# Two tap matmuls for four from a doubly laid pixel buffer, and one convolution block per tile in the small tasks' PSUM banks

## The reference

```python
x = relu(bn(conv3x3(relu(bn(conv3x3(x, sign(w1)))), sign(w2))) + x)      # L0
xn = layer_norm_over_channels(x)                                          # L1: 4 chunks of 16 channels
xz = einsum('gld,ed->gle', chunks, in_proj_w); xi, z = split(xz)
u = silu(causal_depthwise_conv4(xi) + conv_b)
delta = softplus(dt @ dt_proj_w + dt_proj_b)
h = h * exp(delta * A) + (delta * u) * B;  y = h . C                      # scan over 3136 pixels, 16 states
y = (y + u * D) * silu(z);  x = chunks + y @ out_proj_w
x = conv3x3-like block (1x1, grouped 3x3, 1x1) of x + x                   # L2
x = four directional row scans: new = cur + relu(conv9(prev))             # L3
```

## Time and profile before

| | |
|---|---|
| timed runs | median 8,072.02 us of 3 (8,068.12 to 8,075.87) |
| profiled execution | 8,083.31 us, span 8,081.5 us |
| mean granted TensorE clock | 0.943 |
| main loop (224 tiles), between its first and last scan | 707.8 to 7,368.9 us of the span |
| stages A and B, prologue | before 707.8 us |

### The profile page before, as it was taken

One profiled execution on the slowest core, in us unless ns is written; L12 is line 12 of the kernel. 1 busy time (PEld: TensorE's weight loads), 2 busy tenths in 40 slices (PEclk: granted clock), 3 DMA queues, 4 the chain that ended last, 5 costly groups with the idle time before them and its releaser, 6 DMA issues. The chain is left out here.

```text
span 8081.5 us, 108343 instructions
## 1 busy us (share of the span) xinstructions
PE 6926.8 (86%) x31741; PEld 4163.9 (52%) x31741; DVE 6670.6 (83%) x9221; ACT 5321.7 (66%) x9423; POOL 5911.0 (73%) x5627
## 2 busy tenths in 40 slices
PE   8896877878888999999789999999789999996876
PEld 8893333333334555555435555555255555554665
DVE  6776989898989898999889999999898989894111
ACT  0135777777776778777777787777677787773221
POOL 0005989898988888888888888888888888884000
PEclk9998989898989999999989999999899999998999
DMA  9774666565667565656776566656865656565001
GB/s 169 166 179 123 179 166 180 166 178 163 181 173 191 162 164 159 164 165 162 184 194 169 159 166 163 165 157 164 208 172 162 167 159 166 161 164 137 2 2 32
DMA packets 1187366, 1261.38 MB, mean 156 GB/s; under 512 B 475904, under 2 KB 1172992, under 8 KB 1186816
## 3 DMA queue, kind: packets, MB, share of 16 engines
q1 hardware_dynamic: 950784, 1177.89, 54.9%
q10 hardware_dynamic: 236032, 77.08, 4.2%
HBM read 995.47 MB, written 181.59 MB: 146 GB/s over the span
## 5 line engine op out<-in xcount | busy, mean ns | idle before, releaser
L651 POOL TENSOR_TENSOR hs<-hs,bsp 128x448 f32<-128x448 f32 x3584 | 3718.2, 1059 | 411.5 <-DVE hs L641 401.2
L641 DVE TENSOR_TENSOR_SCAN hs<-da,hs,ps 128x448 f32<-128x448 f32 x3072 | 3491.6, 1137 | 0.0
L631 DVE TENSOR_TENSOR ps<-ps,bsp 128x448 f32<-128x448 f32 x3585 | 2200.3, 614 | 368.6 <-PE ps L615 367.9
L621 ACT ACTIVATE da<-da,nega 128x448 f32<-128x448 f32 x3588 | 2252.7, 661 | 51.5 <-issue 37.4
L856 PE MATMUL ps<-pv,ws 128*128 128x224 f32 x8800 | 1882.2, 359 | 218.1 <-DVE pv L920 122.4
L856 PEld LDWEIGHTS ps<-pv,ws 128*128 128x128 f32 x8800 | 1642.4, 190 | 502.3 <-DVE pv L920 202.7
L615 PE MATMUL ps<-stack,seld 96*128 96x448 bf16 x3587 | 1277.6, 370 | 349.4 <-DVE hs L641 260.9
L615 PEld LDWEIGHTS ps<-stack,seld 96*128 96x128 bf16 x3587 | 344.3, 98 | 1328.0 <-DVE hs L641 801.6
L920 DVE SCALAR_TENSOR_TENSOR pv<-ps,R 128x224 f32<-128x224 f32 x880 | 412.5, 469 | 734.6 <-PE ps L856 734.4
L662 PE MATMUL ps<-hs,wc 128*32 128x448 f32 x7200 | 964.2, 589 | 1.5 <-POOL hs L651 1.2
L422 PE MATMUL ps<-xn,wtap 128*128 128x448 f32 x1808 | 857.6, 577 | 9.7 <-ACT xn L526 9.7
(11 more groups left out here) (123 smaller groups left out, 8066.8 us busy)
## 6 DMA issues: line engine op xcount, KB each, us to landing
da<-delta_copy SPq DMA_DIRECT2D x3595, 224.0 KB, 3.8
stack<-parts SPq DMA_DIRECT2D x2700, 28.0 KB, 2.6
delta_copy<-dlt SPq DMA_DIRECT2D x225, 224.0 KB, 1.9
xin<-x_column_pairs SPq DMA_DIRECT2D x224, 145.0 KB, 3.5
x_column_pairs<-otile SPq DMA_DIRECT2D x225, 116.0 KB, 3.1
lnx<-in_x SPq DMA_DIRECT2D x115, 224.0 KB, 2.6
lny<-y_nchw SPq DMA_DIRECT2D x115, 224.0 KB, 2.8
xpad<-in_x SPq DMA_DIRECT2D x64, 392.0 KB, 7.1
```

Of the source, the lines that this page charges most:

```text
L621: a.activation(da[:, j % SLOTS, :], da[:, j % SLOTS, :], ACT.Exp, scale=nega[:, j:j + 1])\
L631: v.tensor_tensor(du, du, bsp[:, st.t % 2, 0, :], ALU.mult).then_inc(S["dbu_done"], 1)
L641: v.tensor_tensor_scan(hs[:, j, 1:T + 1], da[:, j % SLOTS, :], ps[:, DU_BANK + j % 4, 0:T], 0.0 if first else hs[:, j, T:T + 1], ALU.mult, ...
L651: g.tensor_tensor(hs[:, j, 0:T], hs[:, j, 1:T + 1], bsp[:, st.t % 2, 1, :], ALU.mult)\
```

## The change

It has six parts.

1. *Pixels laid twice.* SyncE copies 450 pixels of one image out of `xn` into `xpack`, once into partitions 0 to 63 and once, shifted by one pixel, into partitions 64 to 127 (`pack_pixels`, two DMAs a tile, SBUF to SBUF), for the tile three ahead, in its slot 10. A tap matmul then covers two taps: two matmuls (slots 0 and 2) for four. `z` reads `xpack` too.
2. *One block per tile.* Blocks are no longer placed as events. Each tile has at most one, in TensorE's slot 13, as one more of the small tasks that alternate between the two banks; VectorE evacuates it behind slot 15, SyncE loads and keeps in slot 5. Steps keep `SCNN_BANK` to themselves, and `bank_free` is gone. Three blocks are left for the tail.
3. *Layer norm a tile earlier.* It stands in t 10 to 13 and 0 to 2; in the first pair in 0 to 3 as well as 10 to 13, in the last pair in 0 to 2 alone. The prologue still makes k 0 to 2.
4. *Zero rows of `x3`* are written behind the last load of stage B instead of ahead of stage A's loads.
5. Work for tiles past the end is no longer done (`stands`, and the conditions with `TILES * UN`).
6. The prologue makes two weight products instead of eight, and `pack_p` and `pack_c` are shorter.

```diff
-PE_AT = {0: ["tap0"], 1: ["last3", "tap1"], 2: ["tap2", "tap3"], 3: ["z"], 4: ["project"], 5: ["lnc"], 6: ["bc0"],
-         7: ["dt"], 8: ["sum0", "bc1"], 9: ["lnv"], 11: ["sum1"], 14: ["sum2"]}
+PE_AT = {0: ["tap0"], 1: ["last3"], 2: ["tap1"], 3: ["z"], 4: ["project"], 5: ["lnc"], 6: ["bc0"],
+         7: ["dt"], 8: ["sum0", "bc1"], 9: ["lnv"], 11: ["sum1"], 13: ["blk"], 14: ["sum2"]}
-SP_AT = {2: ["copy"], 8: ["part0"], 11: ["part1"], 13: ["part2"], 14: ["store"]}
+SP_AT = {2: ["copy"], 8: ["part0"], 11: ["part1"], 10: ["pack"], 13: ["part2"], 14: ["store"]}
...
-                self.has_ln = t < 4 or t >= 11
+                soon, late = (3 if p else 4), ST - 4
+                self.has_ln = t < soon or t >= late and p + 1 < PAIRS
+                self.ln_pair = p if t < soon else (p + 1) % PAIRS
+                self.ln_k = t + KT - soon if t < soon else t - late
...
+        for tile in range(TILES):
+            st = Step(tile // ST, tile % ST)
+            for name in TASKS:
+                if name == "blk":
+                    if not BLOCKS_LEFT or tile < tile_of(*BLOCKS_LEFT[0]) + 2:
+                        continue
+                    BLOCK_AT[tile] = BLOCKS_LEFT.pop(0)
+                    TASK_LIST.append((name, BLOCK_NO[BLOCK_AT[tile]]))
+                elif not stands(st, name):
+                    continue
...
-                pe.wait_ge(S["xn_ready"], st.far_xn)
-            a = st.far_k * T + k
-            mm = pe.matmul(ps[:, TMP_BANK + bank, 0:T], wtap[:, st.far_s, k, :], xn[:, a:a + T],
-                           start=(k == 0), stop=(k == 3))
+                pe.wait_ge(packed[st.far % 2], st.far // 2 * 32 + 32)
+            mm = pe.matmul(ps[:, TMP_BANK + bank, 0:T], wtap[:, k, :], xpack[:, st.far % 2, 2 * k:2 * k + T],
+                           start=(k == 0), stop=(k == 1))
...
+        def pack_pixels(sp, tile):
+
+            if tile >= 2:
+                sp.wait_ge(S["tmp_done"], Z_DONE[tile - 2])
+            s, k = tile % ST // KT, tile % KT
+            sp.wait_ge(S["xn_ready"], tile // ST * KT + k + 1)
+            for shift in range(2):
+                sp.dma_start(xpack[C * shift:C * shift + C, tile % 2, :],
+                             xn[C * s:C * s + C, k * T + shift:k * T + shift + T + 2]).then_inc(packed[tile % 2], 16)
...
-        def bank_free(pe, event):
-
-            before = PREVIOUS.get(event)
-            if before is None:
-                return
-            kind, g, n = before
-            if kind == "block":
-                pe.wait_ge(D["cv_evac"], BLOCK_NO[(g, n)] + 2)
-            else:
-                pe.wait_ge(D["row"], g * STEPS + mms_before(n) + 2)
...
@@ sync: stage A, stage B @@
-            sp.wait_ge(D["zeroed"], 1)
-            blank = hs[:, :, :].rearrange("p n f -> p (n f)")
-            for rows in (0, H + 1):
-                sp.dma_start(x3[0:N, :, rows, :].rearrange("n p w -> p n w"),
-                             blank[:, 0:N * (HALF + 1)].rearrange("p (n w) -> p n w", w=HALF + 1))\
-                    .then_inc(D["x3_zeroed"], 16)
             with sp.Fori(0, PAIRS - 1) as i:
                 for b in range(2):
                     sp.wait_ge(sa["split"], i * 2 + (b + 1))
                     load_x(i + 1, b)
-            sp.wait_ge(D["x3_zeroed"], 32)
             barrier(sp, 1)
...
                     sp.dma_start(yin[:, b, :], y1[i * 2 + (2 + b)]).then_inc(sbm[f"in_loaded{b}"], 16)
+            sp.wait_ge(D["zeroed"], 1)
+            blank = hs[:, :, :].rearrange("p n f -> p (n f)")
+            for rows in (0, H + 1):
+                sp.dma_start(x3[0:N, :, rows, :].rearrange("n p w -> p n w"),
+                             blank[:, 0:N * (HALF + 1)].rearrange("p (n w) -> p n w", w=HALF + 1))\
+                    .then_inc(D["x3_zeroed"], 16)
             barrier(sp, 2)
-            for k in range(3):
-                ln_load(sp, Ahead(k))
+            ln_load(sp, Ahead(0))
+            ln_load(sp, Ahead(1))
+            pack_pixels(sp, 0)
+            ln_load(sp, Ahead(2))
+            pack_pixels(sp, 1)
...
+            pack_pixels(sp, 2)
+            sp.wait_ge(D["x3_zeroed"], 32)
@@ sync: a slot of the main loop @@
+                        if j == 5 and st.tile in BLOCK_AT:
+                            load_block(sp, *BLOCK_AT[st.tile])
+                        if j == 5 and st.tile - 1 in BLOCK_AT:
+                            keep_block(sp, *BLOCK_AT[st.tile - 1])
...
+                            elif name == "pack":
+                                if st.tile + 3 < TILES:
+                                    pack_pixels(sp, st.tile + 3)
@@ tensor @@
+                            elif name == "blk":
+                                if st.tile in BLOCK_AT:
+                                    wait_bank(pe, st, name)
+                                    conv_block(pe, *BLOCK_AT[st.tile], TMP_BANK + BANK_NO[(st.tile, name)] % 2)
@@ vector @@
+                        if j == 15 and st.tile in BLOCK_AT:
+                            block_out(v, *BLOCK_AT[st.tile], TMP_BANK + BANK_NO[(st.tile, "blk")] % 2)
```

More of the change, by code:

```diff
@@ L726, in last_of @@
             return 55 * (d + 1)
-        LATE = {"dve": 2, "act": 6, "first": -3, "load": -8, "keep": 8}
+        LATE = {"dve": 2, "act": 6, "first": -3, "load": -8}
         FETCH, STEPS_FROM = 4 * UN, 6 * UN + 4
-        def tile_of(g, b):
-            k, i = b // IMG, b % IMG
-            return (g * GP + i // 2) * ST + i % 2 * KT + min(k + 1, KT - 1)
         def pe_work():
             out = []
-            for t in range(TILES):
+            for tile in range(TILES):
                 for j in range(UN):
@@ L840, in conv_block, with conv_step @@
             mm.then_inc(D["cv_done"], 1)
-        def conv_step(pe, G, m, alone=False):
+        def conv_step(pe, G, m):
             d = direction(m)
-            if not alone and PREVIOUS[("step", G, m)][0] == "block":
-                bank_free(pe, ("step", G, m))
             if m == last_of(d) - 54 + (d >= 2):
@@ L858, in conv_step, with block_out @@
             mm.then_inc(D["mm"], 1)
-        def block_out(v, g, b, bank=SCNN_BANK):
+        def block_out(v, g, b, bank):
             k, i = b // IMG, b % IMG
@@ L1124, in _ @@
             pe.wait_ge(S["wtap_ready"], 1)
-            for k in range(4):
+            for k in range(2):
                 conv_tap(pe, st, k)
@@ L1152, in _ @@
                     for j in range(UN):
-                        spread_du(pe, *unit(st, j + LEAD["du"]))
+                        if st.tile * UN + j + LEAD["du"] < TILES * UN:
+                            spread_du(pe, *unit(st, j + LEAD["du"]))
                         for name in PE_AT.get(j, ()):
+                            if not stands(st, name):
+                                continue
                             if name == "project":
@@ L1178, in _ @@
                 else:
-                    conv_step(pe, g, n, alone=True)
+                    conv_step(pe, g, n)
         @block.scalar
@@ L1305, in _ @@
                         e = event_at(st.tile, j, LATE["act"])
-                        if e is not None and e[0] == "step":
+                        if e is not None:
                             keep_row(a, e[1], e[2])
```

185 lines of the change are left out of this document (82 added, 103 removed).

## The result

| | before | after |
|---|---|---|
| median of 13 runs each, us | 8072.02 | 8099.23 |
| lowest and highest, us | 8063.8 to 8084.7 | 8092.81 to 8105.35 |
| profiled span, us | 8081.5 | 8098.7 |
| mean granted clock | 0.943 | 0.924 |

The ratio is 1.0031, with a 95% interval of 1.0023 to 1.004. Of all executions in this document one, of e7, was disturbed (25,110 us) and is left out of its figures. The profile of before stands 11 us above its median and that of after on its median, so the spans differ by 17 us and the medians by 27. The traces account for the 17.

The account below looks back on a forecast made before the run. The prediction took VectorE as the bound in group 0's plain runs, and VectorE waiting for TensorE in layer-norm runs. Terms -50 - 30 + 8 + 34 - 22 + 10 + 1 - 11 = -60 took 8,072.0 to 8,012 us, range 7,925 to 8,085.

Parts of the forecast that it names:

- The packing DMAs in steady tiles: SyncE's two extra issues a tile land the stack 1.2 us later, mostly hidden: +8 us, bounds 0 and +40.
- The block's move to slot 13: Block in TensorE's slot 13, evacuated 4.8 us later against 2.3 for a block: covered at full clock, no cost summed.
- The first four tiles: In tiles 0 to 3 SyncE's pack waits for pixels made at the tile's end: +34 us, bounds +15 and +45.
- Plain runs: Tiles without layer-norm tasks gain as blocks leave the steps' bank: -50 us, bounds -83 and -25.
- layer-norm runs: Tiles with layer-norm tasks gain from the removed bank waits: -30 us, bounds 0 and -70, likely cap 46.
- Stage A, stage B, prologue: Later zero rows win 22 us in stage A and cost 10 in stage B; the prologue's packing wait costs 1.
- Two taps for four: Halved taps free 320 us of TensorE over 168 tiles, little of it on the path: value by itself 0.
- The ends: Last pair loses three layer-norm tiles at 3.0 us each, the tail one block of 2.3 us: -11 us.
- Rival (a): Less TensorE work lowers the granted clock in groups 1 to 3, making the kernel slower: 8,135 us; chance 0.12.
- Rival (b): Bank waits turn into others, plain runs -25, layer-norm runs 0: 8,067 us, no change; chance 0.17 with its like.
- (c): More comes through: both kinds of run gain 70 and 50, the start costs 20: 7,958 us; chance 0.21 with (d).
- (d): The wait in the first tiles doesn't occur: 7,978 us; chance 0.21 together with (c).

Follow-up runs that it names:

- e7: The kernel before with only the zero rows of x3 moved behind stage B's loads; 8066.09 us, ratio 0.9987.
- e1: The changed kernel with the pack moved in SyncE's queue from slot 10 to slot 1, and to slot 15 in tiles 0 to 3; 8008.07 us.
- e6: The changed kernel with the pack in SyncE's slot 15 in tiles 0 to 3 only, slot 10 otherwise; 8065.1 us.
- e2: The changed kernel with the block in TensorE's slot 12, ahead of the spread that waits for the stack, not slot 13; 8036.48 us.
- e5: The changed kernel with e1's queue order and e2's block slot together; 7974.0 us, ratio 0.9867 to the kernel before.
- e10: e5 with ScalarE's relu moved behind the exponentials of the same tile; 7737.48 us, ratio 0.9586 to the kernel before.
- e12: The changed kernel with only ScalarE's relu moved behind the exponentials of the same tile; 7898.75 us, ratio 0.9781 to the kernel before.
- e11: The kernel before with only ScalarE's relu moved behind the exponentials of the same tile; 7864.26 us, ratio 0.9732.
- e8: e5 with two more tap matmuls in slot 0 of every tile, overwritten by the first true tap; 7973.4 us.
- e3: The changed kernel with two more tap matmuls in slot 0 of every tile, overwritten by the first true tap; 8110.38 us.
- e9: The changed kernel with four taps straight from xn, no packing, and the block in TensorE's slot 12; 7997.5 us.

## Why the prediction was wrong, point by point

The forecast was -60 us, in a range that ended at 8,085; it came out at +27 and above the range. Term by term:

- **The packing DMAs in steady tiles, +8: the step that failed.** e1 against e6, which differ in the pack's place alone, puts them at 57 us by the medians (52 by the ratios, 56 in the table's two middle columns), over the +40 that I had as the bound. Most of it is in the plain runs of groups 1 to 3, 199.4 us on average against 195.0, where I had priced only those of group 0. I had seen the stack 1.2 us late, but reasoned that "the first spread of a tile is wanted by VectorE two to three slots after, which hides it". What I didn't price is what stands behind that spread in TensorE's queue.
- **The block's move to slot 13, +0: the same step from its other side.** I checked the block against its evacuation (2.3 us against 4.8), not against what it had been covering. e2 prices the slot at 63 us. The two overlap: e6 to e5 mends both and is 91 us, less than 57 + 63. That the stack waits would grow in plain tiles was named as a sign that I am wrong.
- **The first four tiles, +34: the mechanism right, the size short.** 48.9 in the trace, against an upper bound of 45. The step "spread and drive 1.0 more: tile 1 starts" left out the tile's last scan and a second product, 1.6 us in each tile; the shift ends 1.1 us later in tiles 1 to 3, and the first block adds 3.3 to tile 3. e6 recovers 34 us by the medians, 47 in its trace.
- **Plain runs, -50, and layer-norm runs, -30.** The term for the banks was sound once the stack was on time: in e5 groups 1 to 3 take 98 us less than before (I had 80 and 9 of the ends), eleven plain runs at 195.0 us on average against 201.1 before, which is 66 us, and 27 in the last pair with its tasks dropped. The layer-norm runs gave almost nothing: 221.3 on average against 222.0, over twelve. (In the changed kernel as it is: 199.2 and 221.1, so 21 us for my 50 and 11 for my 30.) Their limit was neither TensorE nor the bare work of GpSimd, whose busy time I had taken for it, but ScalarE's queue: `u` behind a `relu` that waits for GpSimd. e10 to e12 show this. The 215.4 us that I read as a floor, "without a single row step", fell to 191.4 without any work removed. With that wait gone the change gives the layer-norm runs 44 us (e11 to e12, 12 x 3.7), near the 46 that I had called the cap.
- **Stage A, stage B, prologue, -11 together: right.** The loop starts 15.5 us earlier, and e7 reproduces 15.3 of it. Stage A gives 23.8 (I had 22), stage B takes 8.7 back (I had 10, as two waits; it is one, of 10.11 us for a `y2` store), and the prologue costs nothing where I had 1. By the medians e7 gains 10.
- **Two taps for four, 0: right as to the columns** (e8, and e3 within the intervals). e9 leaves 23 us to the packing that the columns don't explain.
- **The ends:** the tail gave 0.2 us where I had 2. The last pair gave 23.8 (424.3 to 400.5), where its dropped tasks and its share of the 80 come to 16.
- **Rival (a), the clock:** right in sign, wrong as a cause. Its sign was a clock under 0.90 in groups 1 to 3; it is 0.95, and more matmuls raised the clock and not the speed. The Trainium skill ("TensorE: Matmul & The Clock Gate", HAM oscillation — how this bites in real kernels) describes matmul groups that start at the low clock each time because a DMA wait stands between them. The row at 1713.9 agrees for one group, 4.55 us against 2.44. But the clock follows the waits here: with both mends group 0's plain run has 0.92 again in place of 0.84, with no matmul added. Rival (b), that the bank waits turn into others, came true as a mechanism: the waits for the stack took the banks' place, and plain runs gave 21 us and layer-norm runs 11, where (b) had 25 and 0. Its sum missed because group 0 got longer, which no rival had. (c) and (d) didn't occur; the first-tile wait did.

The sum, redone from the table: -15.5 (start of the loop) + 48.9 (first four) - 91.1 (rest of group 0 and groups 1 to 3, as in e5) + 75.0 (the same stages, after against e5) - 0.2 = +17.

## What to carry to other kernels

When an instruction is moved past a wait, price what it used to cover as well as what it now waits for: here a block of 2.4 us had been lying over a transfer's landing, and behind it instead it cost about as much as an added pair of DMA issues. Price an issue in an in-order queue by everything queued behind it. And before a run of tiles is called bound by its busiest engine, follow one head-of-line wait up its queue: the largest gain found here, 236 us from e5 to e10 (227 by the ratios), was one task moved behind five others in ScalarE's order.

## What the runs showed of the hardware

- A wait of 2.81 us of TensorE came with a granted clock of 0.50 for 6.8 us, beginning 0.6 us into the wait and through a block of 12 matmuls that took 4.55 us and not 2.44. At a mean clock of 0.92 to 0.97 such stretches hide well in an average.
- The mean granted clock said little of the time: 0.924 to 0.934 with 11 us more (e3), 0.928 to 0.947 with no change (e8), and e5 with 0.928 is 102 us faster than the kernel before with 0.943.
- Two transfers of tiny packets delayed another queue's store in both places where they stood. In stage B they landed 14.1 and 27.1 us after their issue, and VectorE waited 10.11 us for a `y2` store beside them; the forecast from the `y1` store in the earlier trace rows was 10.
